# Attention by edges on one core: GpSimd waits for each group of four gathers to land before it issues the next

## The reference

```python
k = _typed_linear(x, Wk, ntype); q = _typed_linear(x, Wq, ntype); v = _typed_linear(x, Wv, ntype)
k_e = k[src]; q_e = q[dst]; v_e = v[src]
kw = _typed_rel(k_e, rel_att, etype)
a = (kw * q_e).sum(-1) * rel_pri.T[etype] / sqrt(D)
m = _typed_rel(v_e, rel_msg, etype)
ex = exp(a - segment_max(a, dst)[dst])
attn = ex / segment_sum(ex, dst)[dst]
h = segment_sum(m * attn, dst)
...
# then three times: h = x @ W; agg = segment_sum(h[src] * norm, dst) + b; batch norm
```

## Time and profile before

| | us |
|---|---|
| median of 3 runs | 5087.22 (5078.81 to 5087.94) |
| the profiled execution | 5079.37 |
| its span, first to last instruction | 5077.5 |
| PE busy | 3117.6 (61%) |
| DVE busy | 2306.8 (45%) |
| ACT busy | 1141.3 (22%) |
| POOL busy | 2406.1 (47%) |
| mean granted TensorE clock | 0.784 of full speed |

### The profile page before, as it was taken

How to read it: one execution, slowest core, us unless ns; L and a number is a source line. 1 busy time by engine, 2 the same in 40 slices (tenths; PEclk the granted TensorE clock), 3 DMA queues, 4 the chain that set the end, 5 groups by cost and what they waited for, 6 DMA issues and landing times. The chain is left out here.

```text
span 5077.5 us, 52237 instructions
## 1 busy us (share of the span) xinstructions
PE 3117.6 (61%) x14449; PEld 2234.5 (44%) x14449; DVE 2306.8 (45%) x8186; ACT 1141.3 (22%) x2512; POOL 2406.1 (47%) x2514
## 2 busy tenths in 40 slices
PE   4992666566655555555544208677776777767764
PEld 3772555555555444544432005334443334433432
DVE  4772445445444334443435224554345543445535
ACT  1222454454444433443330021000000000000001
POOL 0004434434444444444435754666636666366662
PEclk9996777777777666666766559988888998899987
DMA  4994544544422122212210006545555555555552
GB/s 110 307 361 140 186 153 170 186 153 166 175 63 59 54 66 64 58 54 65 65 28 1 1 2 216 188 175 189 192 183 178 187 186 181 183 184 182 191 182 82
DMA packets 232026, 706.47 MB, mean 139 GB/s; under 512 B 62326, under 2 KB 111957, under 8 KB 212928
## 3 DMA queue, kind: packets, MB, share of 16 engines
q1 hardware_dynamic: 104252, 447.79, 24.0%
q0 software_dynamic: 93184, 191.21, 12.6%
q10 hardware_dynamic: 34308, 64.13, 3.9%
HBM read 559.66 MB, written 143.28 MB: 138 GB/s over the span
## 5 line engine op out<-in xcount | busy, mean ns | idle before, releaser
L550 POOL DMA_INDIRECT stage<-h_tab,earr x1248 | 1180.0, 946 | 816.9 <-issue 345.4
L525 POOL DMA_INDIRECT arena<-kv_tab,idxr x832 | 805.7, 968 | 1543.6 <-DVE arena L1324 905.6
L1011 PE MATMUL bank<-arena,xr 128*128 128x512 f32 (+1 forms) x2058 | 1023.3, 639 | 4.0 <-issue 4.0
L990 PE MATMUL bank<-oh,stage 128*128 128x128 f32 x2496 | 393.3, 307 | 491.9 <-issue 485.0
L990 PEld LDWEIGHTS bank<-oh,stage 128*128 128x128 f32 x2496 | 353.6, 214 | 707.6 <-issue 695.6
L873 PE MATMUL bank<-oh,stage 128*128 128x128 f32 x1664 | 402.5, 367 | 344.1 <-issue 339.8
L1570 DVE TENSOR_TENSOR sums<-sums,bank 128x128 f32 x1248 | 351.0, 281 | 564.5 <-remote 366.5
L1011 PEld LDWEIGHTS bank<-arena,xr 128*128 128x128 f32 x2058 | 409.0, 212 | 395.4 <-issue 395.4
L641 ACT ACTIVATE arena<-arena,iota_p 128x512 f32<-128x512 bf16 x416 | 276.2, 712 | 1136.4 <-remote 1002.2
L873 PEld LDWEIGHTS bank<-oh,stage 128*128 128x128 f32 x1664 | 328.0, 266 | 417.9 <-issue 415.1
L876 PE MATMUL bank<-oh,arena 128*128 128x128 f32 x1664 | 377.4, 370 | 203.1 <-issue 200.4
(11 more groups left out here) (224 smaller groups left out, 2713.2 us busy)
## 6 DMA issues: line engine op xcount, KB each, us to landing
arena<-a_tab SPq DMA_DIRECT2D x147, 1792.0 KB
a_tab<-stage SPq DMA_DIRECT2D x49, 1792.0 KB
kv_tab<-stage SPq DMA_DIRECT2D x48, 768.0 KB, 8.3
arena<-key_d ACTq DMA_DIRECT2D x52, 512.0 KB, 6.9
arena<-ew_d ACTq DMA_DIRECT2D x52, 512.0 KB, 9.5
arena<-rel_d SPq DMA_DIRECT2D x52, 512.0 KB
stage<-h_tab,earr POOLq DMA_INDIRECT x1248
arena<-kv_tab,idxr POOLq DMA_INDIRECT x832
```

The lines of the kernel that those rows point to most:

```text
L525: G.indirect_dma_start(kv[b % 3][:, t, :], None, kv_tab, bass.IndirectOffsetOnAxis(idxr[:, b % 3, t:t + 1], 0))\
L550: G.indirect_dma_start(gring[:, (q % NG) * GRP + s, :], None, h_tab[l], bass.IndirectOffsetOnAxis(src_i[:, t:t + 1], 0)).then_inc(row_land ...
L990: last = M.matmul(bank[q % NG][:, s * P:(s + 1) * P], gring[:, (q % NG) * GRP + s, :], oh[:, q % NG, s, :], start=True, stop=True)
L1011: mm = M.matmul(o_[:, 0:cw], xr[:, n, :], abuf[B % NBUF][:, n % KB, 0:cw], start=n == 0, stop=n == NT - 1)
```

## The change

Inside a batch, POOL waits ahead of groups 1, 2 and 3 (their scatters and their gathers) until the four gathers of the group in front have landed. The waited count is 64 for each batch that has used this buffer. Nothing else is changed; between batches there is no new wait.

```diff
@@ -515,6 +515,8 @@
                     for j in range(ND):
                         pool.wait_ge(a_zeroed[j], 16 * BPC)
                 for g in range(NG):
+                    if g:
+                        pool.wait_ge(kv_land[b % 3][g - 1], 64 * (b // 3 + 1))
                     for t in slots.get((b, g), ()):
                         scatter(t)
                     if b >= 3:
```

## The result

| | before | after |
|---|---|---|
| median | 5083.0 us (5072.2 to 5087.9, 4 runs) | 4592.9 us (4587.0 to 4594.0, 4 runs) |
| the profiled execution | 5079.4 | 4592.2 |

The ratio is 0.903, with an interval of 0.901 to 0.905: 490 us faster. Forecast were 4670 and a range of 4560 to 5000. So the direction and the mechanism came true, and the time lies 77 us under the forecast, inside the range.

The account below looks back on a forecast made before the run. POOL's chain of indirect DMAs was taken to hold PE's results back. Batch 51 420 us earlier, less 6 lost to the last batch's waits, took 5079.4 to 4665, as a median 4670; range 4560 to 5000.

Parts of the forecast that it names:

- The bound before: Attention part: POOL's chain of indirect DMAs holds PE's results back; steps are POOL's burst plus 17.3 to 17.7 us.
- Price of a quiet wait: POOL, ahead of a group with quiet DMA engines: landing some 3.0 us, so a wait costs 1.75 us.
- The group caught beside the loads: Batches 3 to 25: one group of three likely lands beside large loads, 8.85 us, so its wait costs 7.6.
- POOL's chain as the next bound: Attention part after the change: POOL sets steps of 32 us (batches 3 to 25), 26 (26, 27), 35 (28 on).
- the sum: Whole kernel: 5079.4 less 420 for the earlier batch 51, plus 6 for the last batch's waits, gives 4665 us.
- the start of batch 3: Start of the attention part: three batches with waits take 94 us, so batch 3 starts at 500, 4 us later.
- The runs: Other engines' step: 22.9 us plus what runs exceed 5.4; groups of 4 cost nothing, with scatters 29.3, under POOL's chain.
- The tail: After batch 51: the 48 scatters, tail and layers keep their time; only the last batch's waits add 6 us.
- The signs: Trace: idle before L525 from 1543.6 to under 900, steps 31 to 36 us, 48 scatters near 2120, layers only earlier.
- The hold through the gaps: Between groups: PE's results stay held until a batch's last gather, bursts lengthen; 5330 to 5470, say 5400 us; chance 0.19.
- Long landings: POOL's waits: landings near 5.6 us for every group, steps of 37, 33.4 and 41.2; 4940 us; chance 0.14.
- A toll for each DMA: PE pays 0.91 to 1.03 us per indirect DMA anywhere; waits hide in POOL's idle time; 5080 to 5087; chance 0.07.

Follow-up runs that it names:

- lag2: The change, but POOL waits for the rows of group g-2 instead of g-1, two waits a batch; 5015.6 us, 0.989 of the kernel before.
- pause4: The change with each landing wait replaced by four small additions on POOL, rows not asked for; 4496.9 us, 0.885 of the kernel before.
- every_group: The change plus a fourth wait a batch, ahead of its first group for the preceding batch's last group; 4736.6 us, 0.934 of the kernel before.
- first_half: The change with its waits in batches 0 to 27 alone; 4894.6 us, 0.964 of the kernel before.
- second_half: The change with its waits from batch 28 on alone; 4776.6 us, 0.941 of the kernel before.
- paced_tail: The change, plus the 48 scatters behind the last batch in runs of 6 with 7 landing waits; 4547.7 us, 0.896 of the kernel before.
- pause: The change with each landing wait replaced by three small additions on POOL, rows not asked for; 4538.4 us, 0.894 of the kernel before.
- mid_only: The change with one wait a batch, ahead of the third group, on a chip without the hold; 3982.1 us against 3913.6 before, ratio 1.018.
- the first eight experiments: lag2, pause, first_half and second_half on one chip; every_group, pause4, paced_tail and paced_all on a second; each beside the kernel before.
- paced_all: paced_tail with the next stage's 224 scatters in runs of 6 too, 37 more waits; 4561.3 us, 0.899 of the kernel before.

## Why the prediction was right, and where it was off

On the chips where the kernel before takes about 5075 us:

- **The bound before** (POOL's unbroken run holds the others' results) was right, and is shown by two kernels from both sides: lag2 has the waits and, but for one a batch in the first half, no pause and gains 1%; pause4 has the pause and no wait and gains 11%.
- **Price of a quiet wait**, put at 1.75: the gap is 2.05 in place of 0.30, so 1.75 in the second half. In the first half the two quiet groups show 2.6, so 2.3 each. **The group caught beside the loads**, put at 7.6: gaps of 6.9 to 9.0 in batches 3 to 25, 7.4 on average, so 7.1.
- **POOL's chain as the next bound**, 32, 26 and 35 us: measured 791.4 us for the 25 steps from batch 3 to 28, where 788 was said, and 778.3, 33.8 each, for the 23 behind them, where 805 was said. I had added 1.5 us a step over the worked-out 33.5 for the load of relb; it costs next to nothing. Of the 73 us between the sum, 4665, and the profiled execution this term is 23, and the start of batch 3 at 495.5 instead of 500 is 4.5.
- **The runs** were read wrongly. "The groups of 4 last 4.7 us" and "the runs are 6, 5 and 6 to 7 operations" overlook that no wait stands between two batches: the last group of one and the first of the next make one run of 8, and of 11 with scatters. By the prediction's own measure (22.9 and what each run has over 5.4) the others' step is then 27.2, and 34.1 in the second half, above POOL's 33.5. POOL didn't wait for DVE there at 33.8 us a step, so the others kept within that, and every_group, which breaks these runs, gains nothing. That the sum needed no other bound was luck, by a few tenths of a us.
- **The tail** is the step that failed, and 45 of the 73. "The 48 scatters, the tail of the part and the layers contain no such wait and keep their time", I wrote, and added 6 us for the last batch. From batch 51's first gather to the end it takes 2527.1, where it took 2566.3. The tail isn't a fixed block. Before, DVE had the weighings of batches 49, 50 and 51 to do when batch 51's gathers began, and they took 108.6, 22.9 and 17.3 us. Afterwards DVE is one batch ahead, and only two are left, of 33.6 and 74.9: the 40 us of the two steps behind the held one are gone. first_half has nothing of this gain and second_half 15 us of it, so POOL as the bound of the second half is not enough. paced_tail shows that another 45 us of the tail were the hold itself.
- **The signs.** Steps of 31 to 36 us came true but for batches 26 and 27, with 27 to 30. The idle time before L527 is 970.3 and not under 900, for 405.6 of it is the start of the kernel. The 48 scatters begin at 2095.7, not near 2120, with the whole part.
- **Rivals.** The hold through the gaps: no, L1283 waits 1.5 us in place of 6.35; but in the second half it still waits 4.3, and with a gap of 1.64 us, pause has POOL wait for DVE in every second batch, so the rival stood less than 0.5 us away. Long landings: no, gaps of 2.0 to 3.1 in the second half where it needed 5. A toll for each DMA: no, lag2 and pause4 issue the same DMAs and differ by 519 us (on two chips on which the kernel before differs by 6). There the rule cited from SBUF, Who interferes with whom, of the Trainium skill (DMA never contends with a compute engine) would have meant no change; with the hold it is no guide to when results arrive, and without it the trace agrees (1.0 us of idle time before L1472 in mid_only).

What no step of the prediction had is that all this depends on the chip. The kernel before took some 1160 us more on both chips of the first eight experiments than on the two of the last ones. That all of this is the hold is argued and not shown: no trace of the kernel before was kept on a chip without it. The three cases that I set against the forecast all took the behaviour of the trace as one of every chip. The chips without the hold also came last, and none is known to have been measured twice. Whether it comes from the chips themselves or from something about them at that time, and what in POOL's issuing of indirect DMAs lies behind it, no run here tells.

## What to carry to other kernels

When engines wait for results that the trace shows as long finished, and their waits end only a few us after another engine's long run of small DMA issues, test it with a short busy pause inside that run before believing in a data dependence; and size the pause against the release, since half a microsecond separated all of the gain in the second half (12.2 us a step) from three quarters of it (9.0). A pause that is paid on the bounding engine pays back only while the others are late, so ask after each one what is last then: the freed time of paced_all went into a load behind the last scatter. Measure a change that rests on such a behaviour on more than one chip: this one is worth 490 us on some, and by the estimate above would cost about 425 on others.

## What the runs showed of the hardware that I had not expected

- The same program, instruction for instruction, took 5070 to 5088 us on some chips and 3909 to 3919 on two others; a gather keeps POOL for 957 and 968 ns in the traces of the first kind shown here, and for 953 to 961 in those of the second.
- The hold reaches DVE's waits for its own results too: 50.9 of the 114.0 us before L1472 end with an earlier L1472, and are gone with scatters in runs of 6.
- It goes on in the graph layers. Their gathers in the changed kernel, then in mid_only on a chip without the hold (groups of the page), with 235 us less of idle time on POOL for the same instructions. Of these some 157 are waits for PE's sums (262.7 of "remote" and 27.6 of L992, against 133.0), and 80 are waits for h_tab:

```profile
L552 POOL DMA_INDIRECT stage<-h_tab,earr x1248 | 1183.3, 948 | 810.8 <-issue 346.5
```

```profile
L552 POOL DMA_INDIRECT stage<-h_tab,earr x1248 | 1183.0, 948 | 575.6 <-issue 348.9
```

- On POOL an indirect DMA that follows an addition starts 0.28 us after it if it is a scatter, and 0.81 if it is a gather with the counter steps ahead of it.
